# Byte offsets made once by VectorE for SyncE's row fetches in a four-layer graph network

## The chip, the cores and the metric

One Trainium2 chip, one of its cores. The metric is the device time of one launch in microseconds (us). The kernel is written against the engines directly: TensorE (PE), VectorE (DVE), ScalarE (ACT), GpSimd (POOL) and SyncE (SP) each run a list of instructions of their own, and semaphores tie them together. SyncE has no arithmetic units for tiles: here it issues DMAs, loads numbers into registers and passes semaphores on.

## The reference

Four graph layers follow one another on 6250 nodes with 128 features and 100,000 edges sorted by their target `dst`. Each layer takes rows of a node table by the edges' sources and sums them over the edges of a target:

```python
h = jnp.maximum(_layernorm(x), 0.0)
x = x + _L0_gnn_ref(h, src, dst, ...)     # mean of (h @ W)[src], self edges added
h = jnp.maximum(_layernorm(x), 0.0)
x = x + _L1_gnn_ref(h, ..., edge_weight, src, dst)   # sum of h[src] * weight, two products, normed
h = jnp.maximum(_layernorm(x), 0.0)
x = x + _L2_gnn_ref(h, edge_attr_128, ..., src, dst) # sum of (h @ Wn)[src] * edge network
h = jnp.maximum(_layernorm(x), 0.0)
x = x + _L3_gnn_ref(h, [src, dst], ...)   # attention of 4 heads, softmax over a target's edges
```

What matters here is the part `table[src]`: 100,000 rows of 512 to 532 bytes are fetched from a table in HBM in each of the four layers.

## The kernel before

Edges are taken 128 at a time (a tile), four tiles make a group, and there are 196 groups (`GROUPS`). A ring of 8 groups (`RING`) in the SBUF tensor `work` holds the fetched rows. Each layer writes its table to HBM first: T0 with 129 columns of float32, T1 and T2 with 128, T3 with 133. Then the edge loop of the layer runs on all engines at once.

- GpSimd (`gather_groups`) issues, for each group, up to four gathers of 128 rows each (L683, an indirect DMA). Before group g it waits until SyncE has counted group g - 8 free (`e_free`).
- SyncE (`relay_groups`, L744) walks over the groups n = 0 to 195. In step n it says that the rows of group n + 3 (n + 5 in the last layer) have landed (`ready`, L762), fetches five rows of the side tiles (`fetch_rows`), waits until group n has been used by the consumers, and counts it free for GpSimd (L781). Every fourth step it loads four numbers that tell which count of the consumers to wait for.
- Seven tiles of each layer are taken off GpSimd (`SIDE` = 7). Their 7 x 128 = 896 rows are fetched by SyncE one by one: 5 rows in each step (`SIDE_PER`), into one partition each of a side buffer in `acc` (in the last layer in `work`). When 128 rows are there, `place_rows` (L737) copies the tile into the ring. The source numbers of these rows lie in an input `sides`; `read_sources` (L713) brings 64 of them at a time into one partition, `numbers` (L640) loads five of them into registers, and L728 starts one DMA a row, whose source address depends on the register.
- TensorE multiplies masks with the rows (L1367, in the last layer L1804), VectorE makes the masks and adds the sums (L1401, L1428, L1814), ScalarE runs the edge network and the exponentials. In layers 0 and 1 they also compute the edge network of layer 2.

SyncE works in order: whatever a row fetch takes is spent before the release of the group of that step, and GpSimd waits for this release.

Ahead of the edge loop of layer 0 stands a setup on VectorE (L402 to L524), which makes integer tables from the sorted targets. `rn` is a small tensor that the node stage of layer 0 uses first.

Of the kernel before, what the change touches and what calls it, by code (L numbers as in the profile page):

```python
# [6 lines left out]

F32 = mybir.dt.float32
I32 = mybir.dt.int32
ALU = mybir.AluOpType  # L10
ACT = mybir.ActivationFunctionType
AX = mybir.AxisListType
ENG = mybir.EngineType

N, E, D = 6250, 100000, 128
P = 128
# [10 lines left out]
QUAD = 4  # L27
# [4 lines left out]
SIDE, SIDE_PER, SIDE_READ = 7, 5, 64  # L32
SIDE_BEGIN = [-(-(P * j) // SIDE_PER) for j in range(SIDE + 1)]
SIDE_AT = [SIDE_BEGIN[j + 1] + RING + 2 for j in range(SIDE)]
# [23 lines left out]
ROW3 = HEADS + D + 1  # L58
# [47 lines left out]
def need(engine, *marks):  # L106

    for sem, value in marks:
        engine.wait_ge(sem, value)


def build(nc, a, out):
    with ExitStack() as ctx:
# [6 lines left out]
        def dram(name, shape, dt=F32):  # L120
            return nc.dram_tensor("d_" + name, shape, dt, kind="Internal").ap()

        pe, dve, act, pool, sp = nc.tensor, nc.vector, nc.scalar, nc.gpsimd, nc.sync
        V = Lane(dve, sem("v_done"))
# [36 lines left out]
        tabG = sb("tabG", [P, 3 * TILES])  # L161
        idx, dstf, wgt = tabG[:, 0:TILES].bitcast(I32), tabG[:, TILES:2 * TILES], tabG[:, 2 * TILES:3 * TILES]
        ctl = sb("ctl", [1, 4 * (STEPS + LEAD)], I32)
# [9 lines left out]
        rn = sb("rn", [P, 2, NT])  # L173
# [20 lines left out]
        T0, T1, T2, T3 = dram("T0", [NP, D + 1]), dram("T1", [NP, D]), dram("T2", [NP, D]), dram("T3", [NP, ROW3])  # L194
        scores = dram("scores", [NP, 2 * HEADS])
        windows_b = dram("windows_b", [1, TABB])


        ld_c, ld_w = Load("ld_c"), Load("ld_w")
# [14 lines left out]
        ld_t = Load("ld_t")  # L214
# [13 lines left out]

        ld_g.add(sp.dma_start(lastg, a["lastg"]))
        ld_g.add(sp.dma_start(lastrow, a["lastrow"]))  # L230
        ld_c.add(sp.dma_start(cst[:], a["consts"]))
        steps = hT[:, 4 * TABB:5 * TABB]
        ld_c.add(sp.dma_start(steps, a["steps"].to_broadcast([P, TABB])))
        ld_t.add(sp.dma_start(rawdst, a["dsts"]))
        ld_t.add(sp.dma_start(idx, a["idx"]))
        ld_l.add(sp.dma_start(lastb, a["lasts"].to_broadcast([P, ROWS])))
        ld_t.add(sp.dma_start(wgt, a["wgt"]))
        for k, name in enumerate(("w0", "w1", "w2", "wnT", "we1T", "we2T", "wf1T", "wf2T")):
# [144 lines left out]
        st_0, dv0, nm0 = Load("st_0"), {}, {}  # L383
# [52 lines left out]
        V.did(dve.tensor_scalar(closing2[:], closing2[:], 1, None, ALU.arith_shift_right))  # L436
        V.did(dve.tensor_scalar(ctl3[:, 0:STEPS + 1, 3], slot_s, float(QUAD * ACC3), None, ALU.mult))
        need(dve, ld_t.mark)
        tables = V.did(dve.tensor_copy(dstf, rawdst))


# [82 lines left out]
        prepared = V.did(dve.memset(bcol[:, 7:8], 0.5))  # L524
# [113 lines left out]
        def numbers(engine, view, values, lo, top):  # L638

            _, v = nc.values_load_multi_w_load_instructions(  # L640
                view, engines=[engine], min_val=lo, max_val=top,
                skip_runtime_bounds_check_because="made on the chip from the sorted dst, bounded by the staircase's shape")
            assert len(v) == values
            return v
# [53 lines left out]
        def side_rows(layer, j):  # L698

            lo, width = (MLP + 11 * GRP, ACC3) if layer < 3 else (0, ROW3)  # L700
            return (acc if layer < 3 else work[:, RING * QUAD * ROW3:])[:, lo + j % 2 * width:lo + (j % 2 + 1) * width]

        def side_sources(layer, c):

            row = acc[0:1, NT * ACC3:XC] if layer < 3 else work[0:1, (RING * QUAD + 2) * ROW3:]
            return row[:, c % 2 * SIDE_READ:(c % 2 + 1) * SIDE_READ].bitcast(I32)
# [3 lines left out]

        def read_sources(layer, c):

            sp.dma_start(side_sources(layer, c), a["sides"][0:1, c * SIDE_READ:(c + 1) * SIDE_READ])\  # L713
                .then_inc(s_src[c % 2], 16)

        def fetch_rows(layer, table, n):

            width = table.shape[1]
            for c in range(SIDE_READS):
                lo, hi = [min(max(SIDE_PER * m - SIDE_READ * c, 0), SIDE_READ) for m in (n, n + 1)]  # L720
                if lo == hi:
                    continue
                if lo == 0:
                    sp.wait_ge(s_src[c % 2], 16 * (SIDE_READS // 2 * layer + c // 2 + 1))
                found = numbers(ENG.SP, side_sources(layer, c)[:, lo:hi], hi - lo, 0, N - 1)
                for r, row in zip(range(c * SIDE_READ + lo, c * SIDE_READ + hi), found):
                    j, p = divmod(r, P)
                    sp.dma_start(side_rows(layer, j)[p:p + 1, 0:width], table[bass.ds(row, 1), :])\  # L728
                        .then_inc(s_row[layer][j % 4], 16)
                if hi == SIDE_READ and c + 2 < SIDE_READS:  # L730
                    read_sources(layer, c + 2)
# [824 lines left out]
            return over  # L1556


        over = edge_loop(0, T0, [st_0.mark, ld_t.mark], [st_0.mark, ld_t.mark, prepared, tables])
        for e in (pe, dve, act, pool, sp):  # L1560
            need(e, *over)

# [1 line left out]
        over = edge_loop(1, T1, [st_1.mark], [st_1.mark, cleared[0]])  # L1564
# [15 lines left out]
        over = edge_loop(2, T2, [st_2.mark], [st_2.mark, cleared[1]])  # L1580
# [451 lines left out]
```

## Time and profile before

| | us |
|---|---|
| median of the runs (three: 5316.58 to 5325.49) | 5319.39 |
| span of the profiled execution | 5348.7 |
| PE busy | 2667.0 (50%) |
| DVE busy | 2614.4 (49%) |
| ACT busy | 1816.7 (34%) |
| POOL busy | 2997.4 (56%) |

The profile is of one execution; its span is 29.3 us (0.55%) above the median of the timed runs. Times in the rows are in microseconds from the start of the span unless marked ns. PE is TensorE's matmuls, PEld its weight loads; a q behind an engine's name (SPq) means its sequencer: register, semaphore and DMA-issuing instructions, which are not counted as busy. "<-" before a name tells who ended a wait. L728 is line 728 of the kernel. SPq FUSED_REGOPS is one instruction that holds arithmetic on registers, TENSOR_LOAD loads numbers from SBUF into registers.

### The profile page before, as it was taken

To read this page: it belongs to the slowest core of one execution; us is meant where nothing else is said; L and a number is where in the kernel's file an instruction comes from. 1 tells how busy PE (TensorE), PEld (TensorE's weight loads), DVE (VectorE), ACT (ScalarE), POOL (GpSimd) and SP (SyncE) were. 2 spreads that over 40 slices of the span, in tenths; PEclk is the share of its full clock that TensorE was granted. 3 is DMA by queue.
4 is the path that set the end of the run, shared out by engine and by line. 5 is a ranking of instruction groups with operands and counts; after the bars stand their busy time and mean duration, and the time that the engine had idled before them with its cause. 6 is when DMAs were issued, how large, how long until landed. Compare 5 with 4: busy or idle time off the path is not lost. (4 is left out here: it accounts for less than half of the span.)

```text
span 5348.7 us, 68713 instructions
## 1 busy us (share of the span) xinstructions
PE 2667.0 (50%) x13316; PEld 2230.9 (42%) x13316; DVE 2614.4 (49%) x7231; ACT 1816.7 (34%) x4182; POOL 2997.4 (56%) x3172
## 2 busy tenths in 40 slices
PE   2555555544455555555333333333555555555557
PEld 1444444443344444445333333333444444444446
DVE  3333333333455555546333333333456667767678
ACT  2333333311233333312111111112345555656555
POOL 4556565555556555556355565555345555555553
PEclk7777777766777777767655565656667777767779
DMA  5333333322233333322222222223272111111110
GB/s 113 93 98 100 89 99 97 91 66 54 81 98 91 97 97 90 98 66 56 73 80 82 86 86 82 85 82 87 70 135 48 42 42 42 42 42 42 42 44 25
DMA packets 241787, 405.91 MB, mean 76 GB/s; under 512 B 67715, under 2 KB 140572, under 8 KB 241373
## 3 DMA queue, kind: packets, MB, share of 16 engines
q0 software_dynamic: 99456, 206.27, 15.7%
q10 hardware_dynamic: 74432, 122.18, 8.2%
q1 hardware_dynamic: 67484, 73.06, 4.8%
q8 instruction: 123, 2.02, 0.2%
q14 instruction: 292, 2.38, 0.1%
HBM read 331.63 MB, written 67.78 MB: 75 GB/s over the span
## 5 line engine op out<-in xcount | busy, mean ns | idle before, releaser
L683 POOL DMA_INDIRECT t_work<-d_T,t_tabG x3100 | 2926.8, 944 | 2183.9 <-SPq L781 1098.6
L1367 PE MATMUL ps<-t_work,t_acc 128*128 x2592 | 493.7, 355 | 647.6 <-SPq L762 459.1
L1367 PEld LDWEIGHTS ps<-t_work,t_acc 128*128 128x128 f32 x2592 | 440.9, 258 | 727.1 <-issue 726.7
L1428 DVE TENSOR_TENSOR t_acc<-t_acc,ps 128x128 f32 (+1 forms) x732 | 210.6, 288 | 914.8 <-remote 459.0
L1804 PE MATMUL ps<-t_work,t_hT 128*128 x1960 | 394.5, 363 | 339.0 <-ACT t_hT L1792 157.9
L1417 DVE TENSOR_TENSOR t_hT<-t_work,ps 128x512 f32<-128x512 f32 x244 | 167.2, 685 | 763.7 <-ACT ps L1504 615.0
L1804 PEld LDWEIGHTS ps<-t_work,t_hT 128*128 128x128 f32 x1960 | 337.5, 260 | 406.1 <-issue 406.1
L1367 PE MATMUL ps<-t_hT,t_acc 128*128 128x128 f32 x1296 | 275.2, 399 | 434.6 <-DVE t_acc L1428 313.0
L1504 ACT COPY ps<-t_acc 128x512 f32 x244 | 140.5, 588 | 1022.2 <-SPq L762 723.9
L596 ACT ACTIVATE t_acc<-ps,t_bcol 128x1024 f32<-128x1024 f32 x98 | 109.1, 1113 | 1079.6 <-DVE ps L609 587.4
L1367 PEld LDWEIGHTS ps<-t_hT,t_acc 128*128 128x128 f32 x1296 | 259.5, 306 | 452.6 <-DVE t_hT L1417 295.8
L1367 PE MATMUL ps<-t_work 128*128 x1312 | 247.8, 354 | 323.9 <-SPq L762 212.0
L1714 DVE TENSOR_TENSOR t_hT<-t_work,ps 128x128 f32<-128x128 f32 x980 | 270.9, 281 | 282.6 <-issue 178.6
L1367 PEld LDWEIGHTS ps<-t_work 128*128 128x128 f32 x1312 | 222.6, 258 | 364.6 <-issue 364.5
L1814 DVE SCALAR_TENSOR_TENSOR t_acc<-t_acc,t_hT,ps 128x129 f32 x980 | 336.9, 344 | 68.4 <-remote 56.3
L1726 PE MATMUL ps<-t_cst,t_hT 128*128 128x128 f32 x980 | 204.3, 344 | 249.0 <-DVE t_hT L1714 123.8
L563 PE MATMUL ps<-t_acc,t_wts 128*128 128x512 f32 x392 | 283.1, 864 | 78.8 <-DVE t_acc L602 41.1
L1777 ACT ACTIVATE t_hT<-t_hT 128x128 f32<-128x128 f32 x980 | 310.0, 390 | 0.0
L1792 ACT COPY t_hT<-ps 128x512 f32<-128x512 f32 x245 | 144.3, 589 | 464.7 <-remote 373.1
L572 PE MATMUL ps<-t_wts,t_acc 128*128 128x128 f32 x1568 | 265.4, 341 | 41.0 <-DVE t_acc L617 23.5
L1734 ACT ACTIVATE t_hT<-ps,t_hT 128x128 f32<-128x128 f32 x980 | 273.9, 359 | 32.4 <-remote 31.0
L572 PEld LDWEIGHTS ps<-t_wts,t_acc 128*128 128x128 f32 x1568 | 257.9, 257 | 45.4 <-issue 45.3
(189 smaller groups left out, 4469.0 us busy)
## 6 DMA issues: line engine op xcount, KB each, us to landing
d_edge_net<-t_acc ACTq DMA_DIRECT2D x98, 512.0 KB
t_acc<-d_edge_net SPq DMA_DIRECT2D x98, 512.0 KB
t_work<-d_T,t_tabG POOLq DMA_INDIRECT x3100
t_acc<-in_edge_attrT ACTq DMA_DIRECT2D x96, 512.0 KB
t_acc<-d_T SPq DMA_DIRECT2D x1792, 0.5 KB
t_acc<-d_T SPq DMA_DIRECT2D x896, 0.5 KB
t_work<-d_T SPq DMA_DIRECT2D x896, 0.5 KB
t_acc<-d_T ACTq DMA_DIRECT2D x12, 790.1 KB
```

Of the source, the lines that this page charges most:

```text
L563: last = pe.matmul(ps[:, 4 + h, :], WE1, ein[n % 2][:, h * GRP:(h + 1) * GRP], start=True, stop=True)
L572: last = pe.matmul(ps[:, 6 + k // QUAD, k % QUAD * D:(k % QUAD + 1) * D], sp1[:, k * P:(k + 1) * P], WE2, start=True, stop=True)
L683: pool.indirect_dma_start(out=work[:, at:at + width], out_offset=None, in_=table, in_offset=bass.IndirectOffsetOnAxis(ap=idx[:, g * QUAD + ...
L1367: last = pe.matmul(sums(layer, s, width), masks[s % MASKS][:, k, :], rows_k, start=(k == 0), stop=(k == QUAD - 1))
L1417: dve.tensor_tensor(out=scaled_rows[s % MASKS].rearrange("p (k d) -> p k d", k=QUAD), in0=ring[:, bass.ds(slot, QUAD * ACC3)].rearrange("p ...
L1428: dve.tensor_tensor(out=o, in0=o, in1=sums(layer, s, width), op=ALU.add).then_inc(e_acc[layer], 1)
L1714: ins = dve.tensor_tensor(out=tw[n % 2][:, k * P:(k + 1) * P].rearrange("p (h n) -> p h n", h=HEADS), in0=slots3[:, bass.ds(slots[k], HEAD ...
L1726: last = pe.transpose(ps[:, PT + n % 2, k * P:(k + 1) * P], tw[n % 2][:, k * P:(k + 1) * P], ident)
L1734: last = act.activation(ex[n % 3][:, k * P:(k + 1) * P], ps[:, PT + n % 2, k * P:(k + 1) * P], ACT.Identity, bias=ads[:, QUAD * n + k:QUAD ...
L1777: last = act.activation(e, e, ACT.Exp, bias=run[:, 0, c0 + k:c0 + k + 1], scale=1.0)
L1804: last = pe.matmul(out_of(n, k), pw[n % 2][:, k * P:(k + 1) * P], slots3[:, bass.ds(slots[k] + HEADS, ACC3)], start=True, stop=True)
L1814: dve.scalar_tensor_tensor(out=o, in0=o, scalar=corr[:, n % RINGB, k:k + 1], in1=out_of(n, k), op0=ALU.mult, op1=ALU.add).then_inc(s_add, 1)
```

## The change

The input `sides` is laid out as 128 x 7 and brought once into a corner of `rn`. In the setup VectorE multiplies it three times, by 4 x 129, 4 x 128 and 4 x 133, which gives the byte offset of each row in each kind of table. SyncE stores the three lists into a new HBM tensor `side_at`. From there `read_sources` takes 64 numbers at a time, as it took them from the input. `fetch_rows` sees the table and the side buffer as bytes, so that the number that was loaded is the offset itself. The number of side tiles, of rows a step and the bytes of a row are as before.

```diff
+        side_at = dram("side_at", [3, SIDE * P], I32)
...
+        side_tab = rn[:].rearrange("p j t -> p (j t)")[:, 0:4 * SIDE].bitcast(I32)
+        ld_k, st_k = Load("ld_k"), Load("st_k")
...
+        ld_k.add(sp.dma_start(side_tab[:, 0:SIDE], a["sides"]))
...
         need(dve, ld_t.mark)
+        need(dve, ld_k.mark)
+        for k, width in enumerate((D + 1, D, ROW3)):
+            m_side = V.did(dve.tensor_scalar(side_tab[:, (k + 1) * SIDE:(k + 2) * SIDE], side_tab[:, 0:SIDE],
+                                             float(4 * width), None, ALU.mult))
+        need(sp, m_side)
+        st_k.add(sp.dma_start(side_at.rearrange("k (p j) -> p k j", j=SIDE),
+                              side_tab[:, SIDE:4 * SIDE].rearrange("p (k j) -> p k j", j=SIDE)))
         tables = V.did(dve.tensor_copy(dstf, rawdst))
...
         def read_sources(layer, c):
 
-            sp.dma_start(side_sources(layer, c), a["sides"][0:1, c * SIDE_READ:(c + 1) * SIDE_READ])\
+            k = (layer + 1) // 2
+            sp.dma_start(side_sources(layer, c), side_at[k:k + 1, c * SIDE_READ:(c + 1) * SIDE_READ])\
                 .then_inc(s_src[c % 2], 16)
 
         def fetch_rows(layer, table, n):
 
-            width = table.shape[1]
+            row = 4 * table.shape[1]
+            table_b = table.rearrange("n w -> (n w)").unsqueeze(0).bitcast(U8)
...
-                found = numbers(ENG.SP, side_sources(layer, c)[:, lo:hi], hi - lo, 0, N - 1)
-                for r, row in zip(range(c * SIDE_READ + lo, c * SIDE_READ + hi), found):
+                found = numbers(ENG.SP, side_sources(layer, c)[:, lo:hi], hi - lo, 0, (N - 1) * row)
+                for r, at in zip(range(c * SIDE_READ + lo, c * SIDE_READ + hi), found):
                     j, p = divmod(r, P)
-                    sp.dma_start(side_rows(layer, j)[p:p + 1, 0:width], table[bass.ds(row, 1), :])\
+                    sp.dma_start(side_rows(layer, j)[p:p + 1, :].bitcast(U8)[:, 0:row], table_b[:, bass.ds(at, row)])\
                         .then_inc(s_row[layer][j % 4], 16)
...
-        over = edge_loop(0, T0, [st_0.mark, ld_t.mark], [st_0.mark, ld_t.mark, prepared, tables])
+        over = edge_loop(0, T0, [st_0.mark, ld_t.mark], [st_0.mark, ld_t.mark, st_k.mark, prepared, tables])
```

## Rows read from the trace of the kernel before

**Rows 1.** Busy us and instructions of each engine in the four edge loops, granted clock.

```profile
core 0: us, PE busy (x) PEld busy (x) DVE busy (x) ACT busy (x) POOL busy (x), PEclk, DMA share, GB/s
92.00:1270.00 1178.00, 616.90 (x2942) 499.72 (x2941) 422.88 (x755) 349.33 (x340) 706.14 (x749) 0.72 0.33 88
1350.00:2520.00 1170.00, 649.64 (x3119) 530.26 (x3117) 613.18 (x1025) 362.67 (x421) 694.14 (x735) 0.73 0.31 87
2636.00:3824.00 1188.00, 428.72 (x1978) 396.69 (x1978) 393.09 (x776) 164.72 (x300) 694.64 (x737) 0.60 0.29 84
3954.00:5210.00 1256.00, 706.65 (x3730) 575.38 (x3729) 885.23 (x3771) 740.02 (x2566) 697.12 (x739) 0.76 0.24 49
```

**Rows 2.** Waits, whole span: waiter, releaser, us, times, longest us.

```profile
POOL t_work L683 <- SPq L781: 1098.6, 365, 13.1
...
SPq L781 <- remote: 86.7, 8, 21.5
...
SPq L762 <- DMA t_work<-d_T,t_tabG: 40.6, 11, 6.2
```

**Rows 3.** SyncE's instructions by line, whole span: count, ns min/median/max, first and last start.

```profile
L728 SPq FUSED_REGOPS  x3584: 1/37/1416, 84.8 to 5159.2; - x200
L728 SPq MOVE t_acc<-d_T x2688: 1/29/1452, 85.0 to 3772.3; - x192
L728 SPq DMA_DIRECT2D t_acc<-d_T x2688: 2/225/1435, 85.0 to 3772.3; - x192
...
L640 SPq TENSOR_LOAD <-t_acc x573: 3/1074/3222, 83.7 to 3771.7; - x191
...
L640 SPq TENSOR_LOAD <-t_closing x141: 2/487/1564, 82.7 to 3780.9; - x141
...
L781 SPq EVENT_SEMAPHORE  x752: 2/17/1422, 92.1 to 5209.8; - x188
```

**Rows 4.** The fetch line L728 in 1019 to 1023 us, same columns.

```profile
L728 SPq FUSED_REGOPS  x5: 37/37/37, 1020.9 to 1022.5; - x5
```

**Rows 5.** SyncE's lines in 1005.5 to 1013.6 us, then in 4048.4 to 4057.8 us.

```profile
L728 SPq DMA_DIRECT2D t_acc<-d_T x5: 6/24/703, 1005.4 to 1012.2; - x5
L728 SPq FUSED_REGOPS  x4: 3/20/697, 1005.7 to 1010.1; - x4
L728 SPq MOVE t_acc<-d_T x4: 16/672/715, 1005.8 to 1012.2; - x4
L781 SPq EVENT_SEMAPHORE  x1: 6/6/6, 1012.9 to 1012.9; - x1
L762 SPq EVENT_SEMAPHORE  x1: 717/717/717, 1012.9 to 1012.9; - x1
...
L728 SPq DMA_DIRECT2D t_work<-d_T x4: 17/360/707, 4048.4 to 4056.4; - x4
L728 SPq FUSED_REGOPS  x3: 15/712/727, 4049.1 to 4053.5; - x3
L728 SPq MOVE t_work<-d_T x3: 706/712/712, 4049.2 to 4054.9; - x3
```

**Rows 6.** GpSimd's gathers in order of time: start, us, idle before and who ended it.

```profile
1016.73 0.94 POOL L683 DMA_INDIRECT t_work<-d_T,t_tabG  x1 [0.30 <-issue]
1019.97 0.94 POOL L683 DMA_INDIRECT t_work<-d_T,t_tabG  x1 [2.30 <-SPq L781]
1021.22 0.94 POOL L683 DMA_INDIRECT t_work<-d_T,t_tabG  x1 [0.30 <-issue]
```

**Rows 7.** Other DMAs of SyncE, count, ns min/median/max.

```profile
L713 SPq DMA_DIRECT2D t_acc<-in_sides x42: 3/236/729, 81.9 to 3610.5; - x42
...
L737 SPq DMA_DIRECT2D t_work<-t_acc x21: 3/483/712, 286.6 to 3775.2; - x21
...
L1981 SPq DMA_DIRECT2D out<-t_x x15: 345/372/388, 5271.7 to 5345.1; - x15
```

**Rows 8.** DMA of 1930 to 1936 us (layer 1): queue, packets; issues by line.

```profile
q1 hardware_dynamic: 10, 0.00, 0.2%
...
t_acc<-d_T SPq DMA_DIRECT2D x5, 0.5 KB
```

**Rows 9.** The setup in order of time: VectorE, then SyncE.

```profile
38.20 0.15 DVE L404 TENSOR_SCALAR t_acc<-t_acc 128x2 int32<-128x2 int32 x1
...
75.08 0.16 DVE L478 TENSOR_TENSOR t_small<-t_cst,ps 128x8 f32<-128x8 f32 x1 [23.23 <-remote]
...
13.88 0.43 SPq L236 DMA_DIRECT2D t_acc<-in_lasts x1
```

More of the change, by code:

```diff
@@ L9 @@
 I32 = mybir.dt.int32
+U8 = mybir.dt.uint8
 ALU = mybir.AluOpType
@@ L2007 @@
         "lastg": lastg.reshape(2, P).T, "lastrow": lastg[:GROUPS].reshape(1, GROUPS),
-        "sides": np.concatenate([src[QUAD * g + QUAD - 1] for g in SIDE_AT]).reshape(1, SIDE * P),
+        "sides": np.concatenate([src[QUAD * g + QUAD - 1] for g in SIDE_AT]).reshape(P, SIDE),
         "idx": src[:TILES].T, "dsts": dst[:TILES].T, "wgt": weight[:TILES].T,
```

## The prediction

> **What bounds the kernel now.** I read the four edge loops first, because they hold 4792 of 5349 us [rows 1]. No engine is full in them: GpSimd's gathers are busy 694 to 706 us of some 1180, and the largest other share is VectorE's 885 of 1256 us in the last layer. So something makes them wait, and the list of waits names it: GpSimd stands 1098.6 us, 365 times, before a gather until SyncE's L781 has counted a group free [rows 2]. The same list says what SyncE waits for itself, and there is almost nothing: 86.7 us in 8 times before L781 and 40.6 us for landed gathers, of nearly 4800 us [rows 2]. SyncE is thus always working or held up at its own instructions, and it is the bound of all four loops. 188 groups are released in each, so one step takes 1178/188 = 6.27 us in layer 0 (layers 1 and 2: 6.22 and 6.32, I take 6.27 for the three) and 1256/188 = 6.68 us in layer 3 [rows 1]. GpSimd could do a group in four gathers of 1.25 us, 5.0 us [rows 6].
>
> **What a step of SyncE is made of.** A row fetch is three instructions, FUSED_REGOPS (37 ns), MOVE (29 ns) and the DMA's issue (225 ns) [rows 3]. In an undisturbed stretch five of them start between 1020.9 and 1022.5 us, one in 0.41 us [rows 4]; 0.12 us of that are three gaps, some 0.04 us each. A step is five fetches (2.05 us), one TENSOR_LOAD of 1.07 us, a quarter of one of 0.49 us, and two semaphore instructions with all gaps (0.2 us): 3.45 us, for 5 x 3 + 1 + 0.25 + 2, with side cases 18.4, instructions [rows 3]. But a step takes 6.27 us. The rest is a second mode: between 1005.5 and 1013.6 us 15 instructions of SyncE take 8.1 us, in layer 3 10 take 9.4 us, and a MOVE or a register instruction, which took 29 or 37 ns, now takes 0.7 us as often as a DMA does [rows 5]. Call it 0.7 us an instruction whatever its kind (between 0.54 and 0.94). The gathers set when this mode comes: the quick stretch at 1020.9 us follows a pause of GpSimd and its first new gather at 1019.97 us [rows 6], and the slow ones lie where gathers follow each other.
>
> With 18.4/3.45 = 5.33 instructions/us in the quick mode and 1/0.7 = 1.43 in the slow one, the slow time Ts of a step follows: 18.4 = 1.43 Ts + 5.33 (6.27 - Ts), so Ts = 3.85 us, of 5.0 us in which GpSimd gathers. In layer 3 Ts = 4.4 us.
>
> **The change part by part.** *Removed:* the two multiplications of an offset (by the row's width and by 4) are the content of the FUSED_REGOPS of L728, 3584 of them [rows 3], one a fetch. I expect them all to go, since a byte offset with a step of one byte needs no arithmetic; MOVE and the DMA stay. The step then has 13.4 instructions and in the quick mode takes 3.45 - 5 x 0.08 = 3.05 us, 4.39 instructions/us. Four gathers a group stay, so I keep Ts. 13.4 = 1.43 Ts + 4.39 (P - Ts) gives P = 3.05 + 0.674 Ts: 5.65 us in layers 0 to 2 (0.62 less), 6.02 us in layer 3 (0.66 less). 896 rows are 180 steps a layer: 180 x (3 x 0.62 + 0.66) = **454 us**.
>
> The bounds of the term. From above: if the mode follows the number of instructions as a whole, the step keeps 18.4/6.27 = 2.93 instructions/us, takes 13.4/2.93 = 4.6 us, and GpSimd's 5.0 us bind; that is 180 x (3 x 1.27 + 1.68) = 988 us. From below: 0.08 us a fetch and nothing of the slow mode is 5 x 0.08 x 720 = 288 us; if the slow mode is tied to DMAs alone, the register instruction is hidden while it lasts and only the quick part of the step gives, 288 x (1 - 3.85/6.27) = 111 us. I take 454, since rows 5 show register instructions stretched as often as DMAs.
>
> *What is late next:* GpSimd at 5.0 us, VectorE in layer 3 at 885.23/188 = 4.7 us of work a group [rows 1]; both stay under the 5.65 and 6.02 us.
>
> *Moved and added:* L713 reads the same 64 numbers from another HBM tensor, nothing. In the setup SyncE issues one more load, 0.43 us as L236 beside it, behind which later loads slide; SyncE has them out long before they are needed. VectorE gets three operations on 128 x 7 numbers, 0.15 us each as L404, in front of `tables`, and a wait for a load that was issued some 30 us earlier. They are hidden by VectorE's own wait of 23.23 us before L478; without that cover they cost 0.5 us [rows 9]. SyncE's new wait for VectorE comes at about 46 us; behind it on SyncE stand the store of the windows and the first edge loads, which wait for VectorE's later work (after 75 us) anyway. The store of `side_at` has 30 us to land, so its mark at the loop is met. Sum of the setup: 0, at most 0.5 to 1 us.
>
> *The access itself:* the row stays one run of 512 to 532 bytes, but its elements are 516 bytes instead of 129 floats. If that makes the issue dearer, 0.225 us could become 0.372 (L1981) or 0.483 us (L737), the next dearer forms of SyncE's DMAs; a form of int32 costs 0.236 us (L713), so the type alone seems not to matter [rows 7]. I take 0 extra.
>
> Here a rule speaks for more pieces. In layer 1 five fetches of 128 floats make 10 packets on the queue, two a fetch, data and semaphore [rows 8]. The Trainium skill, DMA: Bandwidth & Descriptors, section "Why a DMA increments its semaphore by 16 and not by 1", says that a copy is split over the largest number up to 16 that divides its slowest dimension; 128 floats would then already be 16 pieces, and the bytes of all tables 12 to 16. The trace does not agree for these rows, so by it nothing is to be expected from the byte view.
>
> **The rivals.**
> *A. The modes grow apart less than I assume (small gain).* Slow time is bought by DMAs, or a busier GpSimd brings more slow time: 111 to 288 us less, time 5040 to 5210. For it: the last bound above, and that GpSimd, with less idle time, is in the slow mode longer. Against it: rows 5. Chance 0.20.
> *B. The slow time shrinks with the instructions (large gain).* 600 to 988 us less, 4340 to 4720. For it: stretches of 0.7 us fall on all kinds alike. Against it: in the slow stretches the pace seems set from outside. Chance 0.15.
> *C. Slower: the issue of a byte row is dearer.* With d us more a fetch the step's quick time is 3.05 + 5d; it decides from d = 0.21 us, where P is 6.27 again. At L737's price, d = 0.26: P = 6.41 us in layers 0 to 2 and 6.71 in layer 3, 540 x 0.14 + 180 x 0.03 = 81 us more, 5400. Against it the 0.236 us of the int32 rows and the unchanged bytes. Chance 0.07.
> *D. No effect.* Either the build still puts a register instruction before each DMA (a multiplication by one), which leaves FUSED_REGOPS at 3584, or the slow mode belongs to the recorded execution alone and SyncE is no bound without it. The second is spoken against by the times: with SyncE at 3.45 us a step GpSimd would bind at 5.0 us, some 1000 us less than the 5319.39 that the timed runs took, while span and median differ by 0.55%. The Trainium skill, NOTIFIC — the notification-queue block, section 7.1, has a rule for it: records of the profiler can hold up the engine that makes them; no run here shows yet whether it does. Chance 0.08, 5319.
>
> **How the numbers follow.** The sum is made on the span: 5348.7 - 454 = 4895 us. The median of the runs is 0.9945 of the span, so 4868, I say 4870 us. The forecast (4720 to 5040) has the chance 0.50, A 0.20, B 0.15, C 0.07, D 0.08. For 8 in 10 the range takes in the forecast, nearly all of A and half of B: 4600 to 5190 us. A measurement here can tell about 0.2%; faster than that has 0.50 + 0.20 + 0.15 = 0.85, within it 0.08, slower 0.07.
>
> **What the profile after would show.** FUSED_REGOPS of L728 gone and SyncE's instructions 3584 fewer; MOVE and DMA at 29 and 225 ns in the median. If the issue's median is over 0.43 us, C holds. The steps (loop length over 188) near 5.65 and 6.0 us, GpSimd's idle time before gathers down by about the gain and still ended by L781; if its gathers follow at 1.25 us without waits, B holds. A slow stretch should still cost 0.5 to 0.9 us an instruction; if it costs more an instruction and the same a fetch, the mode is tied to DMAs (A). SyncE waiting long at L781 would show that the consumers have become the bound. What would make the prediction wrong is the split between the two modes: it rests on two windows and on the assumption that Ts stays.

## The result and the profile after

The changed kernel takes 5286.95 us (median of 6 runs, 5282.23 to 5303.68), the kernel before 5321.6 us beside it (6 runs, 5316.58 to 5325.49). The ratio is 0.9947, with an interval of 0.9931 to 0.9964: 0.5% faster, 35 us. I had forecast 4870 us with a range of 4600 to 5190. The direction is right and the size is wrong by a factor of about 13.

The profiled execution has a span of 5280.9 us, against 5348.7 us. The four edge loops, in the windows of the first and the last release of each layer (columns as in [rows 1]):

```profile
core 0: us, PE busy (x) PEld busy (x) DVE busy (x) ACT busy (x) POOL busy (x), PEclk, DMA share, GB/s
106.50:1220.00 1113.50, 600.26 (x2932) 475.14 (x2932) 421.09 (x752) 347.64 (x340) 694.30 (x734) 0.71 0.35 93
1297.70:2446.80 1149.10, 622.18 (x3093) 499.72 (x3092) 607.97 (x1017) 361.16 (x413) 701.90 (x742) 0.73 0.31 89
2557.60:3704.10 1146.50, 426.79 (x1978) 395.74 (x1978) 391.87 (x776) 163.94 (x298) 700.74 (x742) 0.60 0.30 87
3840.30:5143.40 1303.10, 755.03 (x3730) 615.48 (x3731) 904.42 (x3772) 740.33 (x2568) 699.08 (x739) 0.72 0.23 48
```

The time from the first to the last of a loop's 188 releases, over the 187 intervals between them, is the step. It went from 6.28, 6.23, 6.35 and 6.72 us (the releases of before lie within 5 us of the edges of [rows 1]) to 5.95, 6.14, 6.13 and 6.97 us. So layers 0 to 2 gave 119 us and layer 3 took 47 back. The four loops together went from 4784 to 4712 us. This is 72 us for one execution of each kernel, and their spans differ by 68 us, where the medians of the timed runs differ by 35: the shifts by layer hold to some 30 us. The first release came later, at 106.5 us instead of 92.1. That is not the setup: x_static below, without the change, has 105.6 us.

SyncE's fetches, now line 742, and its load of the five numbers (L652, which was L640), as count, ns min/median/max, first and last start:

```profile
L742 SPq MOVE t_acc<-d_T x2688: 2/29/1411, 86.9 to 3658.1; - x192
L742 SPq DMA_DIRECT2D t_acc<-d_T x2688: 2/228/1432, 88.3 to 3658.2; - x192
L742 SPq MOVE t_work<-d_T x896: 4/29/1424, 3823.0 to 5086.8; - x180
L742 SPq DMA_DIRECT2D t_work<-d_T x896: 5/225/1432, 3823.0 to 5086.9; - x180
...
L652 SPq TENSOR_LOAD <-t_acc x573: 3/728/2856, 85.4 to 3657.7; - x191
```

VectorE's three multiplications of the setup in the groups of instructions (busy us, mean ns, idle before):

```profile
L446 DVE TENSOR_SCALAR t_rn<-t_rn 128x7 int32<-128x7 int32 x3 | 0.3, 151 | 0.0
```

All 3584 FUSED_REGOPS of [rows 3] are gone, MOVE and DMA have kept their medians, and the operations of the setup cost what was said. So the change does on SyncE just what I had taken it to do. But GpSimd's wait for SyncE (L695 is the gather, L795 the release, L776 the wait for landed gathers), which I had wanted to see fall by about the gain, hardly moved from the 1098.6 us of [rows 2]:

```profile
POOL t_work L695 <- SPq L795: 1030.2, 305, 10.9
...
SPq L795 <- PE ps L1818: 158.0, 55, 11.3
SPq L795 <- remote: 118.7, 26, 21.2
...
SPq L776 <- DMA t_work<-d_T,t_tabG: 46.3, 12, 6.5
```

SyncE waits at its own release for longer: 158.0 us for TensorE's scatter of layer 3 (L1818), and 118.7 us for "remote". Before it was 86.7 us for "remote" [rows 2] and for the scatter, then L1804:

```profile
SPq L781 <- PE ps L1804: 21.1, 6, 6.2
```

"remote" stands for a wait whose end no record of the trace explains. All waits at the release together went from 137 to 329 us, which is what the prediction had named as the sign that the consumers have become the bound.

### The profile page after: what moved, and what is told of

It is laid out like the page before. It is cut to its first block, busy times and chain, and to the rows that moved or that the text cites. A ratio compares the mean times of both kernels' runs of the same rounds, so it can differ in the third digit from the quotient of the medians.

```text
span 5280.9 us, 65135 instructions
## 1 busy us (share of the span) xinstructions
PE 2674.6 (51%) x13316; PEld 2219.1 (42%) x13316; DVE 2632.6 (50%) x7234; ACT 1815.0 (34%) x4182; POOL 3008.2 (57%) x3172
## 3 DMA queue, kind: packets, MB, share of 16 engines
q14 instruction: 263, 2.15, 0.1%
## 4 chain that ended last, share of the span: by engine, by line
SPq 27%; issue 26%; another core or an unknown queue 17%; DVE 11%; ACT 10%; PE 7%; DVEq 2%; POOL 1%; DMA 0%; ACTq 0%; POOLq 0%
SPq L742 16%; SPq L652 8%; ACT t_hT L1791 3%; PE ps L1818 3%; ACT t_hT L1748 3%; SPq L776 2%; DVE ps L1415 1%; PE ps L1799 1%; SPq L795 1%; DVEq L652 1%; DVE t_acc L1423 1%; ACT t_hT L1806 1%; SPq L766 1%; DVE t_acc L1442 1%
## 5 line engine op out<-in xcount | busy, mean ns | idle before, releaser
L695 POOL DMA_INDIRECT t_work<-d_T,t_tabG x3100 | 2936.0, 947 | 2111.9 <-SPq L795 1030.2
L1381 PE MATMUL ps<-t_work,t_acc 128*128 x2592 | 464.7, 335 | 465.4 <-issue 217.1
L1381 PEld LDWEIGHTS ps<-t_work,t_acc 128*128 128x128 f32 x2592 | 422.8, 245 | 538.3 <-issue 537.7
L1818 PE MATMUL ps<-t_work,t_hT 128*128 x1960 | 415.3, 377 | 266.2 <-ACT t_hT L1806 139.6
L1818 PEld LDWEIGHTS ps<-t_work,t_hT 128*128 128x128 f32 x1960 | 356.4, 272 | 338.4 <-issue 338.4
L575 PE MATMUL ps<-t_acc,t_wts 128*128 128x512 f32 x392 | 312.0, 942 | 229.2 <-DVE t_acc L614 194.1
L1740 PE MATMUL ps<-t_cst,t_hT 128*128 128x128 f32 x980 | 223.4, 369 | 321.0 <-remote 152.5
L1381 PE MATMUL ps<-t_work 128*128 x1312 | 228.7, 332 | 272.5 <-SPq L776 116.7
L1740 PEld LDWEIGHTS ps<-t_cst,t_hT 128*128 128x128 f32 x980 | 144.2, 184 | 388.6 <-remote 165.4
L584 PE MATMUL ps<-t_wts,t_acc 128*128 128x128 f32 x1568 | 241.9, 319 | 69.6 <-DVE t_acc L629 52.4
L584 PEld LDWEIGHTS ps<-t_wts,t_acc 128*128 128x128 f32 x1568 | 230.0, 233 | 81.8 <-issue 80.9
```

Of the source, the lines that this page charges most:

```text
L575: last = pe.matmul(ps[:, 4 + h, :], WE1, ein[n % 2][:, h * GRP:(h + 1) * GRP], start=True, stop=True)
L584: last = pe.matmul(ps[:, 6 + k // QUAD, k % QUAD * D:(k % QUAD + 1) * D], sp1[:, k * P:(k + 1) * P], WE2, start=True, stop=True)
L695: pool.indirect_dma_start(out=work[:, at:at + width], out_offset=None, in_=table, in_offset=bass.IndirectOffsetOnAxis(ap=idx[:, g * QUAD + ...
L1381: last = pe.matmul(sums(layer, s, width), masks[s % MASKS][:, k, :], rows_k, start=(k == 0), stop=(k == QUAD - 1))
L1740: last = pe.transpose(ps[:, PT + n % 2, k * P:(k + 1) * P], tw[n % 2][:, k * P:(k + 1) * P], ident)
L1818: last = pe.matmul(out_of(n, k), pw[n % 2][:, k * P:(k + 1) * P], slots3[:, bass.ds(slots[k] + HEADS, ACC3)], start=True, stop=True)
```

## The experiments

Every kernel below raises each count that an engine reads from a table and then waits for to at least 1 in a register. The two with nothing else changed are the bases. The ratio is always to the unchanged kernel before, run beside it on the same chip. The kernel before did not run alike everywhere. In the measurement of the result it took 5322 us, on chips 3 and 1 5263 and 5323 us, and on chips 2, 14 and 11 4183, 4182 and 4184 us. The number of the first chip isn't on record; it may be chip 1 again, so the slower kind was met three times on at least two chips. I call it **chips with stalls** and the other **chips without stalls**; why is shown below.

### The bases, and SyncE without its registers or its fetches (a chip with stalls, before 5262.74 us)

The edit of the bases, and the two edits of the fetch on the base of before:

```
 edge, win, off, slot = numbers(...)
+edge = smax(edge, 1)          # and so for each number that is waited for

x_static
-found = numbers(ENG.SP, side_sources(layer, c)[:, lo:hi], hi - lo, 0, N - 1)
-    sp.dma_start(side_rows(layer, j)[p:p + 1, 0:width], table[bass.ds(row, 1), :])
+    sp.dma_start(side_rows(layer, j)[p:p + 1, 0:width], table[r:r + 1, :])

x_nofetch
-    (loads, row DMAs and the wait for them)
+sp.dma_start(work[:, at:at + width], table[P * j:P * (j + 1), :])   # in place_rows
```

> The kernel before, in which every count that an engine reads from a table and then waits for is first raised to at least 1 in a register. Nothing that is computed changes. SyncE gets one register instruction more a step (752 in all), TensorE 488, VectorE 245, ScalarE 244. It is the base of the experiments, and a test of the prediction's price: at 0.12 us of a step for one instruction (0.62 us for five, as I had it) it is 752 x 0.12 = 93 us slower, some 5413 us. At the price that the result shows, 35 us for 3584 instructions, it is 7 us slower, some 5329.

Measured: 5262.28 us, ratio 1.000 (0.9984 to 1.0017). 752 more instructions on SyncE cost nothing that can be seen, where the prediction's price gave 93 us.

> The kernel after with the same register instructions. If they are neutral it stands to its base as after to before, 0.995 of it, some 35 us less. If the gain depends on how close SyncE is to its limit it is another: with one instruction more a step the modes theory of the prediction still wants over 400 us between the two.

Measured: 5233.74 us, 0.9939 (0.9918 to 0.9960). The result of the change stands again, 29 us, and not 400.

> Base before, but the side rows are fetched from addresses fixed in the program (row r for r): no table of sources is read into registers. Leaves out the right choice of the rows. SyncE loses five FUSED_REGOPS, five MOVE and one TENSOR_LOAD of 1.07 us a step and keeps its five DMAs; the quick step would be about 1.6 us instead of 3.45, the instructions 7.4 instead of 18.4. Slow mode at 0.7 us per instruction (the prediction): the step falls under GpSimd's 5.0 us, some 900 to 1000 us less. Slow mode tied to DMAs or to time: only the quick part goes, 1.83 x (1 - 3.85/6.27) = 0.7 us a step, 500 us less, 4820. If SyncE's own length is not what bounds the loops at all: less than 100 us less.

Measured: 5164.59 us, 0.9806 (0.9773 to 0.9839), 98 us less. Its step: 5.82, 6.01, 6.02, 6.87 us. Eleven of 18 instructions of a step are gone, its longest load among them, and 98 us less is, just, the expectation's third case: SyncE's own length is not what bounds the loops.

> Base before without the side rows' fetches: no load of sources, no MOVE, no register operation and no DMA for them; the side tile is filled by one copy of 128 rows at a fixed place. Leaves out the right rows of seven tiles. A step of SyncE is two semaphore instructions and a quarter of a load. If SyncE's step is the bound of the loops (both the prediction and the view that the slow mode is tied to DMAs), GpSimd's four gathers of 1.25 us must bind next: 5.0 us a step, 188 x 4 x 1.3 = 980 us less, 4340 us, and GpSimd waits for SyncE no more. If the consumers or a common cause hold all engines, the time stays over 5100 us and SyncE then waits long for the consumers' counts.

Measured: 5146.38 us, 0.9774 (0.9742 to 0.9807), 116 us less. This is the run that decides. SyncE's waits in it:

```profile
SPq L781 <- remote: 1883.1, 164, 28.1
SPq L781 <- PE ps L1806: 695.0, 118, 16.1
SPq L781 <- DVE t_hT L1419: 614.3, 88, 23.7
SPq L781 <- PE ps L573: 180.6, 36, 6.0
SPq L762 <- DMA t_work<-d_T,t_tabG: 70.8, 23, 6.2
...
SPq L781 <- PE ps L1369: 66.7, 12, 12.8
```

SyncE has next to nothing to do and stands 3440 us (the five lines of L781) waiting for consumers. Yet the steps are 5.90, 6.01, 6.21 and 6.69 us, against 6.16, 6.14, 6.20 and 6.61 us of the base. In layers 2 and 3 they are not shorter at all. GpSimd's 5.0 us never bind: it still stands 946.6 us before its gathers until SyncE's release. So right behind SyncE stands a second limit, between 5.9 and 6.7 us, and all that was to be had here by taking away SyncE's fetches altogether is 116 us.

What holds the consumers is seen in the same run in order of time (start, us, engine and line; in brackets the idle time before and who ended it):

```profile
598.50 2.02 PE L573 MATMUL ps<-t_wts,t_acc 128*128 128x128 f32 x16 [0.36 <-DVE t_acc L618]
...
600.36 1.61 PE L1369 MATMUL ps<-t_work,t_acc 128*128 x12
...
602.42 0.19 PEld L1369 LDWEIGHTS ps<-t_work,t_acc 128*128 128x128 f32 x1 [0.74 <-issue]
...
603.13 0.19 PEld L1369 LDWEIGHTS ps<-t_work,t_acc 128*128 128x128 f32 x1 [0.53 <-issue]
...
604.54 0.19 PEld L1369 LDWEIGHTS ps<-t_work,t_acc 128*128 128x128 f32 x1 [1.23 <-issue]
...
605.26 0.19 PEld L1369 LDWEIGHTS ps<-t_work,t_acc 128*128 128x128 f32 x1 [0.53 <-issue]
605.97 0.27 PE L1369 MATMUL ps<-t_work,t_acc 128*128 x1 [1.05 <-issue]
...
613.87 0.72 DVE L1430 TENSOR_TENSOR t_acc<-t_acc,ps 128x129 f32 x2 [14.20 <-remote]
```

TensorE loads and starts twelve matmuls in 1.6 us, and the next weight loads follow at distances of 0.71 or twice 0.71 us, waiting for nothing that the profile shows. That is the 0.7 us that I had seen on SyncE [rows 5]. VectorE's addition for the pair of groups whose last matmul (of L573) ends at 600.5 us starts at 613.87. It is TensorE's count that comes late, and not VectorE: in the trace the semaphore which this matmul counts up changes at 613.75 us, and SyncE's release, which waits for the same count, follows at 613.76. GpSimd gathers without a pause from 597 to 611 us meanwhile.

### No side tiles, bytes in three layers, fewer gathers, more instructions

The four edits (the second and the last on the base of after):

```
x_side0    -return min(QUAD, ET - QUAD * g) - (g in SIDE_AT)
           +return min(QUAD, ET - QUAD * g)          # and no fetches, no placing
x_b012     +numbers as before and table[bass.ds(at, 1), :] where layer == 3
x_gath3    +return min(QUAD, ET - QUAD * g) - (g in SIDE_AT or g >= RING)
x_sem2     +for _ in range(2): sp.sem_inc(s_spare, 1)   # ahead of each row's DMA
```

They met a chip without stalls first (before 4183.12 us), while the expectations were written for one with stalls. So these four runs show what happens without stalls and leave the expectations untested.

> Base before without side tiles at all: GpSimd gathers the seven last tiles of their groups too, 28 gathers more in all, and SyncE fetches nothing. Everything that the reference asks for is computed. The run without fetches gained 116 us although SyncE then waited 3440 us for consumers, so I expect the same here less what 28 gathers of 1.25 us cost: nothing where GpSimd waits for its groups anyway, 35 us where it doesn't. 5146 to 5181 us, faster than both kernels. If SyncE's step were the bound it would be 4340 us; if the side tiles are worth more than their fetches cost, it is over 5262.

Measured: 4217.0 us, 1.0081 (1.0067 to 1.0095), 34 us slower.

> Base after, but layer 3 fetches its rows by number as before (FUSED_REGOPS back in that layer alone, 896). In the two traces layers 0 to 2 became 118 us shorter and layer 3 became 47 us longer. If the loss of layer 3 is caused by its own fetches having become quicker, this run is some 40 to 50 us under base after (5190 us). If layer 3's length only goes with how its stalls happen to fall, or is handed on from the layers ahead, it stays where base after is, 5234, within 10 us.

Measured: 4183.04 us, 1.0002 (0.9993 to 1.0011).

> Base before, but from the ninth group on GpSimd gathers three tiles of a group and leaves the fourth as an earlier group left it; the fourth tile's rows are wrong. 720 gathers fewer (a quarter). If the slow mode, in which an instruction takes 0.7 us, comes with the gathers and their traffic, whoever is held by it (SyncE, TensorE) is held a quarter less: of 3.85 us a step in the slow mode 0.96 us go over into the quick one, and the loops get 0.7 us x 752 = 500 us shorter or more, under 4760. If the slow mode belongs to the instructions themselves (their number, or the records made of them), the time stays within 100 us of 5262, since GpSimd was waiting anyway.

Measured: 3654.39 us, 0.8744 (0.8730 to 0.8758), 529 us less.

> Base after, with two semaphore instructions more ahead of each fetch (7168 in all, on a semaphore that nobody waits for; about 0.07 us each with its gap in the quick mode). A step has 23.4 instructions. By the prediction's 0.12 us of a step an instruction (0.7 us in the slow mode) this costs ten of them, 1.2 us a step, 720 steps: 880 us, 6110. By the quick cost alone 0.14 us a fetch is 500 us at the most where SyncE is the bound all the time. By the price that after against before showed, 35 us for 3584 instructions, it is 70 us, 5305; but the curve should steepen when instructions are added, since SyncE then is the last to be ready, so I expect 150 to 400 us.

Measured: 4184.35 us, 1.0006 (0.9997 to 1.0016). 7168 instructions more cost nothing.

Then three of them and the base of after met a chip with stalls (before 5322.99 us).

> Base after once more, in whichever of the two conditions that the runs have shown comes up: loops held by stalls of 0.7 us (the kernel before at 5263 us, 0.994 of it with the change), or loops without them (before at 4183 us, where SyncE waits 1328 us for landed gathers in the run with bytes in three layers). Without the stalls I expect no difference, 1.000 within 0.002, since GpSimd's gathers of 1.25 us, four a group, set the pace at 4.95 us a step and SyncE has time to spare. With them 0.994 again.

Measured: 5314.11 us, 0.9988 (0.9978 to 0.9998), 9 us and not the 0.994 expected. The base of before wasn't run on this chip, so what the added register instructions cost here isn't known; on chip 3 it was nothing.

> The kernel without side tiles again. Without the stalls it was 0.8% slower: 28 gathers more at 1.25 us are 35 us, and it was 34. With the stalls I expect it near the run without fetches, 0.977, at most the 35 us more, 0.984: faster than the kernel before there, slower than it here. That would make the side tiles a choice that is right only where the stalls don't come.

Measured: 5254.78 us, 0.9871 (0.9856 to 0.9886), 68 us faster than the kernel before. So it beats the kernel before and the base of after where the stalls come and loses to them where they don't, as the expectation had it; the ratio lies just above its 0.984. SyncE waits 3475 us at its release there (1911.7, 753.1, 648.0 and 162.0 us by who ended it), and the steps are 5.86, 6.10, 6.37 and 6.87 us: the second limit once more, on another chip.

> Base after with two semaphore instructions more ahead of each fetch again. Without the stalls they changed nothing (1.0006). With the stalls: 0.14 us a fetch of quick time on SyncE, and by the prediction's own rule 1.2 us a step, 6110 us. The result of the change itself, 35 us for 3584 instructions, gives 70 us over base after, 0.994 + 0.013 = 1.007. I expect 1.01 to 1.06, since SyncE becomes the last again in layer 3.

Measured: 5491.03 us, 1.0312 (1.0297 to 1.0327), 177 us over the base of after beside it. Ten instructions a step cost 0.21 us a step in the mean of the four layers (6.37, 6.53, 6.47 and 6.90 us against 6.08, 6.22, 6.16 and 6.97), not 1.2. Layer 3 pays nothing.

> Three gathers a group from the ninth on again (the fourth tile keeps an earlier group's rows, so its sums are wrong). Without the stalls it was 0.874, 529 us less, of 720 gathers x 1.25 = 900 us. With the stalls: if they come with the gathers' traffic the time falls by at least as much, to 0.87 or under; if they come with the number of instructions and their records, GpSimd was not the bound and the time falls by less than 100 us, over 0.98.

Measured: 4454.6 us, 0.8378 (0.8363 to 0.8392), 868 us less, 1.2 us for each of the 724 gathers left out. The windows of its loops:

```profile
92.00:1045.00 953.00, 569.73 (x2938) 464.85 (x2936) 421.87 (x754) 349.36 (x340) 538.50 (x570) 0.77 0.37 97
1123.00:2082.00 959.00, 602.93 (x3113) 491.13 (x3113) 610.34 (x1020) 362.28 (x421) 526.25 (x556) 0.78 0.33 94
2196.00:3159.00 963.00, 422.63 (x1978) 390.19 (x1978) 392.56 (x775) 166.62 (x300) 526.52 (x558) 0.62 0.32 92
3286.00:4310.00 1024.00, 656.19 (x3732) 527.50 (x3732) 887.76 (x3770) 744.02 (x2566) 529.69 (x560) 0.83 0.24 49
```

GpSimd's wait for the release:

```profile
POOL t_work L689 <- SPq L787: 1185.6, 488, 11.7
```

The steps are 5.10, 5.13, 5.15 and 5.47 us with SyncE's work unchanged. GpSimd itself was waiting, and still is, so the gain isn't its own time: everybody else gets on faster when there are fewer gathers. The stalls come with the gathers. Whether with GpSimd's instruction or with the DMA traffic that it starts isn't separated by this run.

### The same change where there are no stalls

> Bytes in layers 0 to 2, layer 3 by number, where the stalls come. In two pairs of traces (before and after, the two bases) layer 3 was 47 us longer with bytes. If its own quicker fetches are the cause, this run is 40 us or more under base after of the same call (a ratio lower by 0.008) and its layer 3 has a step near 6.6 us. If not, the two are within 10 us and its layer 3 keeps 6.9 us.

Measured: 4184.51 us, 1.0007 (0.9998 to 1.0016), on a chip without stalls (before 4182.35 us), as the next three runs, which stood beside it.

> Base after, beside the run with bytes in three layers alone. So far 0.9939 and 0.9988 of before on two chips with stalls. I expect 0.994 to 0.999 where they come, 1.000 where they don't, and in layer 3 a step of 6.9 us (with them).

Measured: 4185.13 us, 1.0006 (0.9997 to 1.0015). The change is worth nothing there, and its setup costs nothing that can be seen: the first release comes at 77.0 us, and at 77.5 us in x_gath3, which lacks the setup. The profile says why. The fetch, now L748:

```profile
L748 SPq MOVE t_acc<-d_T x2688: 29/29/38, 75.2 to 2979.6; - x192
L748 SPq DMA_DIRECT2D t_acc<-d_T x2688: 217/228/1057, 75.3 to 2979.7; - x192
```

The waits (L701 is the gather, L801 the release, L782 the wait for landed gathers):

```profile
POOL t_work L701 <- issue: 903.3, 2956, 1.7
...
POOL t_work L701 <- SPq L801: 46.5, 141, 1.7
...
SPq L782 <- DMA t_work<-d_T,t_tabG: 1393.0, 676, 6.8
```

And the four loops by window:

```profile
77.00:1009.00 932.00, 573.74 (x2974) 470.42 (x2972) 426.27 (x773) 352.47 (x347) 704.29 (x748) 0.78 0.42 112
1077.00:2001.00 924.00, 600.93 (x3131) 488.43 (x3129) 612.38 (x1025) 362.83 (x421) 698.70 (x740) 0.78 0.39 111
2096.00:3019.00 923.00, 417.35 (x2041) 388.88 (x2040) 401.26 (x801) 172.56 (x310) 698.04 (x739) 0.64 0.38 109
3124.00:4050.00 926.00, 588.21 (x3740) 469.32 (x3738) 886.41 (x3772) 742.88 (x2569) 695.95 (x738) 0.91 0.32 67
```

The longest MOVE of 2688 is 38 ns, where it was 1411 ns. SyncE waits 1393 us for landed gathers, GpSimd only 46.5 us for SyncE, and the step is 4.98, 4.94, 4.94 and 4.96 us: GpSimd's floor, four gathers of 1.25 us.

> No fetches of side rows and three gathers a group from the ninth on (base before; the side tiles and the fourth tiles hold other rows than they should). SyncE has nothing to do but count. Where the stalls come: if the consumers are held by the gathers' traffic, as SyncE is, their steps of 5.9 to 6.7 us without fetches fall with the gathers by about a quarter, to some 4.6 to 5.2 us, and the run is at 0.80 to 0.83. If the consumers have a length of their own that has nothing to do with the gathers, it stays over 0.95. The first also means that removing SyncE's work altogether is worth as little with three gathers as with four, 0.01 to 0.03.

Measured: 3562.76 us, 0.8516 (0.8503 to 0.8529). It met no stalls, so it does not tell what it was made for. But it shows the consumers' own length without stalls: with no fetches and three gathers a group the steps are 3.81, 4.05, 3.78 and 4.83 us, so the consumers need no more than that for the same work for which they need 5.90 to 6.69 us in x_nofetch on a chip with stalls. In layer 3 the 4.83 us can't be GpSimd's three gathers (3.75 us): there the consumers stand close under the four gathers' 5.0 us even without stalls.

> Base after, in which layer 3's groups are told ready six steps ahead of their release instead of five. SyncE waited 131 us there for TensorE's scatter. If that wait is the consumers' having been told late, they have one step more and the wait and some 40 us go; the cost is that SyncE waits for landed gathers instead, 6 steps x 7 us = 42 us after a group's release, with eight groups in the ring. If the consumers are held by themselves, no change within 10 us, or slower because SyncE waits for the gathers in front of the fetches.

Measured: 4250.68 us, 1.0162 (1.0147 to 1.0178). Without stalls the earlier notice costs 66 us: layer 3's step is 5.29 us instead of 4.96, and GpSimd's wait for SyncE rises from 46.5 to 111.5 us. That is the price that the expectation named, SyncE standing at a wait for gathers with the fetches and the release behind it. What it does with stalls wasn't seen.

> Bytes in layers 0 to 2, layer 3 by number, once more. Without the stalls 1.0005 again. With them, if layer 3's own quicker fetches make it longer: its step near 6.6 us instead of 6.9 and a ratio of 0.986 to 0.991 to before. If not, 0.994 to 0.999 as base after, and a step of 6.9 us.

Measured: 4183.76 us, 1.0002 (0.9993 to 1.0011), once more on a chip without stalls (before 4184.45 us).

> No fetches and three gathers a group, once more (side tiles and fourth tiles hold other rows). Without the stalls 0.852 again. With them: 0.80 to 0.83 if the consumers are held by the gathers' traffic (a step of 4.6 to 5.2 us instead of 5.9 to 6.7), over 0.95 if they have a length of their own.

Measured: 3563.01 us, 0.8512 (0.8499 to 0.8525), likewise. Layer 3's loss and the consumers under fewer gathers stay untested where it matters.

## Why the prediction was wrong, point by point

**What is right.** The two multiplications were the whole content of FUSED_REGOPS, and all 3584 went. MOVE (29 ns) and DMA (228 ns) stayed, so rival C is out. The setup is free: 1.0006 on a chip without stalls holds all of it. The quick mode's price is of the right size, as the count below shows. And GpSimd's floor of 5.0 us a step is real, 4.94 to 4.98 us where there are no stalls.

**The step that failed: "SyncE is the bound of all four loops" and, behind it, "what is late next: GpSimd at 5.0 us".** I had read the bound from the list of waits: SyncE waited for almost nothing [rows 2], so it had to be the only limit. That is right for one step ahead only. How far behind the next limit stands can't be seen in that list, and I priced it with the quick length of the other engines' work: 5.0 us of gathers, 4.7 us of VectorE. But the other engines were running under the same stalls. With SyncE emptied the consumers still need 5.9 to 6.9 us a step (x_nofetch, and x_side0_r on another chip), where the base with SyncE's full work has 6.14 to 6.61: 4% less in layer 0, 2% in layer 1 and nothing in the others. Of the 454 us at most 116 were to be had. Without stalls VectorE's 4.7 us for layer 3 was a fair price for the consumers, 4.83 in x_ng3.

**The mis-sized term: "0.7 us an instruction whatever its kind" and "I keep Ts".** A held item is here an instruction of SyncE, or a gap between two, of 0.64 to 0.76 us (or within 0.06 us of twice or three times 0.71). At least three of them, each less than 1 us behind the one before, make a held stretch. What is left of the loops is the quick part:

| trace | loops, us | held, us (instructions in it) | us each | us a DMA | quick, us |
|---|---|---|---|---|---|
| before | 4784 | 2741 (4421) | 0.62 | 2.17 | 2043 |
| after | 4712 | 2917 (3811) | 0.77 | 2.03 | 1795 |
| base_b | 4695 | 2600 (4548) | 0.57 | 2.09 | 2095 |
| base_a | 4654 | 2907 (4142) | 0.70 | 1.96 | 1747 |
| base_a_r | 4756 | 3004 (4019) | 0.75 | 2.15 | 1752 |
| x_sem2_r | 4912 | 2535 (4690) | 0.54 | 2.35 | 2377 |
| x_gath3_r | 3899 | 1473 (2961) | 0.50 | 1.87 | 2426 |
| base_a_s (no stalls) | 3706 | 0 | - | - | 3706 |

Before the change this is 3.6, 3.5, 3.2 and 4.3 us a step in the four layers, so Ts (3.85 and 4.4) was read about right. The step's 18.4 instructions are 17.7 in the trace (13312 over 752 releases), which matters little. In the quick part the change gives 248 us (before to after), and 348 between the bases, on either side of my price of 288 us for 3584 instructions, though SyncE's longer waits at its release are counted in what is left. The held part takes 176 of the 248 back: it grows from 2741 to 2917 us although it holds fewer instructions. Between the bases it takes back 307 of 348 us, and with instructions added it goes the other way, 469 of 625 us. So Ts is no constant: a SyncE that is quicker between its stalls spends more time in them, and seven tenths to nine tenths of what the quick part gains go there. And a removed instruction didn't take its time along: the time per instruction rose from 0.62 to 0.77 us (0.57 to 0.70 between the bases), while that per DMA hardly moved (2.17 to 2.03, and 2.09 to 1.96). That is what I had named as the sign of rival A. The exact figures hang on where a stretch is said to end. The direction doesn't: the held items alone, without the stretches, add up to 2707 us before and 2872 after, 2552 and 2851 for the bases, and 2969 (base_a_r) and 2483 with instructions added.

**The two are one thing.** A quicker SyncE only meets consumers that are later. Between the start of the last matmul of a pair of groups, which counts the pair as done, and the start of VectorE's addition of that pair lie in the mean of the 122 pairs of layers 0 and 1 (us, from the instructions' starts in the traces):

| trace | layer 0 | layer 1 |
|---|---|---|
| before, after | 3.47, 5.21 | 3.80, 5.38 |
| base_b, base_a | 3.44, 5.02 | 3.87, 5.65 |
| base_a_r, x_sem2_r | 4.91, 2.57 | 5.59, 3.28 |
| x_static, x_nofetch, x_side0_r | 6.10, 5.96, 6.26 | 6.37, 6.32, 6.59 |
| x_gath3_r | 1.79 | 2.85 |
| base_a_s (no stalls) | 0.62 | 2.26 |

Some of it is VectorE's own order of work, above all in layer 1 (2.26 us without stalls). The rest goes one way: the less SyncE has to do, the longer TensorE's results wait to be taken up, and with fewer gathers or no stalls they wait less. So what the change takes from SyncE comes back as time held on SyncE and as delay behind TensorE. How it is shared between the two, and why a stall falls on the one or the other, is not shown.

**The rivals.** A had the mechanism: slow time that stays or grows, and a time per instruction that rises. But its price, 111 to 288 us, still lies over the measured 35. B is out on the chips with stalls, though its end (GpSimd at 5.0 us) is what holds without them, for both kernels alike. D's first half is out. Of its second half the argument from the times was wrong: I said that GpSimd would bind some 1000 us lower if the slow mode weren't real. It does, 1080 to 1140 us lower, on three chips with the same recording. So the slow mode is no property of the kernel, nor of being recorded as such. It goes with the chip (each was met once, so chip and moment aren't separated), or with how that chip takes the records. The Trainium skill, NOTIFIC — the notification-queue block, section 7.1, says that inside the block a full pipeline holds its producers rather than lose a record. Stalls of a fixed 0.71 us that fall on many engines' instructions would fit that. So would a second thing: where the stalls come, records are missing. Of the 752 changes of the semaphores that SyncE's release counts up the trace of after holds 542 and that of before 599, but that of base_a_s holds 750. No run here was without recording, so it is open. It also means that "remote" in a wait list of a chip with stalls can be a change that was not recorded.

**A reading without consequence.** The prediction found that the trace contradicts the rule of the Trainium skill on the pieces of a copy (DMA: Bandwidth & Descriptors, section "Why a DMA increments its semaphore by 16 and not by 1"). It doesn't. The rule goes by the dimensions as the instruction carries them, and in both traces the fetch carries its row as 1 x 1 elements of 512 to 532 bytes, so there is nothing to split, and the 10 packets of five fetches [rows 8] agree with it. Floats and bytes come out the same; in the kernel after five fetches (1915 to 1921 us) make 10 packets too.

**Layer 3.** It became longer in both pairs of traces from chips with stalls: 6.72 to 6.97 us and, between the bases, 6.61 to 6.86. It was 6.87 us in x_static and x_side0_r as well, 6.69 in x_nofetch. So its length doesn't follow SyncE's work. What grew there is SyncE's wait for TensorE's scatter, from 21.1 to 158.0 us. With it went TensorE's granted clock, 0.76 to 0.72 in the layer, and PE's busy time, 706.65 [rows 1] to 755.03 us. Which is cause and which effect stays open: the runs meant for it (x_b012 three times, x_ahead) met chips without stalls.

## What to carry to other kernels

An engine that never waits is the first limit, but what relieving it is worth is decided by the second one; its length must be read under the same disturbance, or measured by one run in which the first engine's work is taken away altogether (here 116 us of 454 promised). Where short instructions take a fixed 0.7 us now and then, compare their longest duration on another chip before pricing anything with it. A kernel that spends idle instructions of one engine to save another's can win on one chip and lose on the next: against the kernel before, leaving out the side tiles costs 34 us without stalls and gains 68 us with them.

## What the runs showed of the hardware

The same kernel ran at 5263 to 5323 us in three measurements (chips 3 and 1 and the one of the result) and at 4182 to 4184 us in three others (chips 2, 14 and 11), about 21% less, with the same busy time of GpSimd in the loops (2797 us without stalls, 2796 after with them). The difference is waiting, much of it with no releaser that the trace could name. Two samples from the kernel after, first a slow stretch (500 to 510 us), then a quick one (3008 to 3013 us):

```profile
L742 SPq DMA_DIRECT2D t_acc<-d_T x5: 13/697/746, 500.0 to 510.0; - x5
L742 SPq MOVE t_acc<-d_T x4: 5/356/725, 500.7 to 509.3; - x4
...
L742 SPq DMA_DIRECT2D t_acc<-d_T x9: 190/218/252, 3007.9 to 3011.8; - x9
L742 SPq MOVE t_acc<-d_T x8: 29/29/29, 3008.1 to 3011.8; - x8
```

The same two instructions need 10 us for five fetches in the one and 4 us for nine in the other. On chip 1, with stalls, each gather left out was worth 1.2 us of the whole although GpSimd waited for SyncE over 1000 us: with a quarter of the gathers gone SyncE was held 1473 us, where it is 2535 to 3004 us in the traces with all gathers and all fetches, and TensorE's results were passed on sooner, after 1.79 us in layer 0 instead of 2.6 us and more. A fetch row from a tensor of bytes costs SyncE the same issue as one from a tensor of floats, 228 and 225 ns.
